# Two buffers for the forward decays of a state-space mixer, one in PSUM and one in SBUF, and a shared place for the turned gated output

## The reference, cut to what matters

```python
dt = softplus(einsum('blr,dr->bld', dt, dt_w) + dt_b)   # 256 channels
A = -exp(A_log)                                          # 256 channels x 16 states
dA = exp(dt[..., None] * A)                              # the decays
dBx = dt[..., None] * Bm[:, :, None, :] * xc[..., None]
# for each token: h = dA_t * h + dBx_t ; y = sum over the 16 states of h * C_t
y = (ys + xc * D) * silu(z)                              # the gated output
out = einsum('ble,ed->ble', y, out_w)
```

## Time and profile before

| | |
|---|---|
| median of 3 runs | 3504.08 us (3494.14 to 3508.31) |
| profiled execution | 3522.14 us, its span 3520.3 us |
| mean granted TensorE clock | 0.891 |
| busy over the span | PE 77%, DVE 73%, ACT 63%, POOL 60% |
| mixer's scans | about 1500 to 3122 us of the span |
| busy in the mixer | about 9 tenths for DVE, ACT and POOL in the page's slices, 8 for PE |

### The profile page before, as it was taken

The page is one execution under the profiler, slowest core; times in us unless marked ns, Lnnn a source line. Parts: engine busy times, 40 slices in busy tenths (PEclk is TensorE's granted clock), DMA queues, the critical chain, the costliest instruction groups (busy, mean ns, idle before and its releaser), DMA issues. The chain is left out here.

```text
span 3520.3 us, 56028 instructions
## 1 busy us (share of the span) xinstructions
PE 2719.5 (77%) x18635; PEld 2086.9 (59%) x18635; DVE 2575.9 (73%) x3474; ACT 2232.3 (63%) x3991; POOL 2114.0 (60%) x1427
## 2 busy tenths in 40 slices
PE   3999999322999920688888888888888887749994
PEld 2555555221999920256666666666666665639993
DVE  3788887443333357089999999999989999967893
ACT  1577776320222200498899898889989989746652
POOL 1233332464333312389998899898989989832565
PEclk6799999555999965799999999999999999879995
DMA  4455554212666654012222222222222222212222
GB/s 105 91 102 100 106 100 79 73 55 85 192 191 192 193 151 102 31 62 73 82 76 79 75 76 72 79 80 75 78 74 77 73 77 82 84 54 76 67 61 75
DMA packets 221906, 321.69 MB, mean 91 GB/s; under 512 B 37706, under 2 KB 133478, under 8 KB 216874
## 3 DMA queue, kind: packets, MB, share of 16 engines
q1 hardware_dynamic: 200322, 298.46, 30.6%
q0 software_dynamic: 12224, 18.29, 1.5%
q10 hardware_dynamic: 9072, 1.27, 0.3%
HBM read 269.84 MB, written 55.68 MB: 92 GB/s over the span
## 5 line engine op out<-in xcount | busy, mean ns | idle before, releaser
L1720 POOL TENSOR_TENSOR resid_x<-s_ux,s_B_rows 128x1024 f32<-128x1024 f32 x256 | 605.4, 2365 | 141.9 <-PE s_y L2080 141.3
L2000 DVE TENSOR_TENSOR_SCAN resid_x<-s_dA,resid_x 128x1024 f32<-128x1024 f32 x256 | 581.1, 2270 | 126.7 <-ACT s_dA L1811 123.4
L2008 DVE TENSOR_TENSOR_SCAN resid_x<-s_back_decay,s_back_in 128x1024 f32<-128x1024 f32 x256 | 583.4, 2279 | 55.5 <-ACT s_back_decay L1821 55.5
L2080 PE MATMUL s_y<-identity,resid_x 128*128 128x128 f32 x4096 | 553.9, 280 | 7.2 <-issue 6.4
L2080 PEld LDWEIGHTS s_y<-identity,resid_x 128*128 128x128 f32 x4096 | 493.8, 145 | 58.4 <-issue 36.0
L1728 POOL TENSOR_TENSOR resid_x<-resid_x,s_C_rows 128x1024 f32<-128x1024 f32 x192 | 454.5, 2367 | 4.0 <-DVE resid_x L2000 4.0
L2067 PE MATMUL s_back_in<-identity,resid_x 128*128 128x128 f32 x2048 | 293.1, 290 | 141.5 <-ACT resid_x L1832 74.1
L491 DVE TENSOR_REDUCE a_row_max<-a_maxscores 128x2 f32<-128x512 f32 x512 | 335.9, 684 | 87.9 <-PE a_maxscores L566 87.3
L2015 DVE TENSOR_TENSOR resid_x<-resid_x,s_C 128x1024 f32<-128x1024 f32 x320 | 382.3, 1195 | 14.0 <-PE s_C L2057 10.6
L1811 ACT ACTIVATE s_dA<-s_dt,s_A 128x510 f32<-128x510 f32 x512 | 330.0, 676 | 87.7 <-DVE resid_x L2000 87.5
L1832 ACT ACTIVATE resid_x<-s_uT,s_bT 128x256 f32<-128x256 f32 x864 | 368.8, 498 | 1.3
(11 more groups left out here) (391 smaller groups left out, 5349.2 us busy)
## 6 DMA issues: line engine op xcount, KB each, us to landing
s_B_rows<-forward_rows SPq DMA_DIRECT2D x256, 256.0 KB, 3.1
e_w<-L_ffn_w_by_expert SPq DMA_DIRECT2D x71, 768.0 KB, 4.8
s_C_rows<-forward_rows SPq DMA_DIRECT2D x192, 256.0 KB
a_Q<-split_qk SPq DMA_DIRECT2D x96, 192.0 KB
split_qk<-a_parts SPq DMA_DIRECT2D x32, 384.0 KB, 2.7
e_x<-slot_inputs SPq DMA_DIRECT2D x71, 130.0 KB
a_K<-split_qk SPq DMA_DIRECT2D x64, 128.0 KB
c_y<-choice_outputs SPq DMA_DIRECT2D x16, 512.0 KB, 6.7
```

What stands on the lines that cost most here:

```text
L1720: tt(R[s, 0], ux[par][:], brow[s % BRING][:].unsqueeze(1).broadcast_to([P, C2, W]), ALU.mult).then_inc(S["in_ready"], 1)
L2000: nc.vector.tensor_tensor_scan(r, a, r, 0.0, ALU.mult, ALU.add).then_inc(S["scanned"], 1)
L2008: nc.vector.tensor_tensor_scan(r[:, ::-1], a[:, ::-1], b[:, ::-1], 0.0, ALU.mult, ALU.add).then_inc(S["scanned"], 1)
L2080: last = mm(YP[:, t, c2 * P:(c2 + 1) * P], R[s, d][:, c2, t * P:(t + 1) * P], core.ident[:], is_transpose=True, start=((s, d) == (0, 1) an ...
```

## The change

The forward decays get two buffers, used in turn by even and odd states: the PSUM tile as before for even states and a new SBUF tile for odd states. ACT may now write the decays of a state once the forward scan of two states before has read that buffer. The first column of both buffers is set to zero at the start. The place for the new SBUF tile (4 KB in each partition) comes from `ygT`, which now lies in `ex`; so ACT's copies into `ygT` get one more wait, on the last read of that half of `ex` by POOL in the current pair (`off_corr`). The order of the instructions on each engine is the same as before, but for one more memset on DVE before the loop.

```diff
--- before.py
+++ after.py
@@ -1633,9 +1633,9 @@
         R = {(s, d): lots[:, 4 + s % 2 if d else s % 4] for s in range(DS) for d in range(DIRS)}
         bt = [core.X[:, k * C2 * W:(k + 1) * C2 * W].rearrange("p (n e) -> p n e", e=DI) for k in (6, 7)]
         yg = sb("y_gated", [P, G * TC, DI])
-        ygT = sb("y_gated_T", [P, C2, W])
+        ygT = ex
         o = sb("out", [P, G * TC, D])
-        dA = core.psum("s_dA", [P, C2, G, T], on=on)
+        dA = [core.psum("s_dA0", [P, C2, G, T], on=on), sb("dA1", [P, C2, G, T])]
         bP = core.psum("s_back_in", [P, C2, G, T], on=on)
         YP = core.psum("s_y", [P, G * TC, DI], on=on)
         CP = core.psum("s_C", [P, W], on=on)
@@ -1658,7 +1658,8 @@
             @block.vector
             def _(dve):
                 nc.vector.memset(xT[:], 0.0)
-                nc.vector.memset(dA[:, :, :, 0:1], 0.0)
+                for n in range(2):
+                    nc.vector.memset(dA[n][:, :, :, 0:1], 0.0)
                 nc.vector.memset(dec[0][:, :, :, T - 1:T], 0.0)
                 nc.vector.memset(dec[1][:, :, :, T - 1:T], 0.0).then_inc(S["pads"], 1)
                 dve.wait_ge(S["pads"], 1)
@@ -1806,9 +1807,9 @@
 
                     if s == 0:
                         act.wait_ge(S["dt_ready"], DIRS * C2 * j + C2)
-                    at(act, S["scanned"], CHUNKS * j + (2 * s - 1))
+                    at(act, S["scanned"], CHUNKS * j + (2 * s - 3))
                     for c2 in range(C2):
-                        last = func(dA[:, c2, :, 1:T], dt[par][:, 0, c2, :].rearrange("p (g t) -> p g t", t=T)[:, :, 1:T],
+                        last = func(dA[s % 2][:, c2, :, 1:T], dt[par][:, 0, c2, :].rearrange("p (g t) -> p g t", t=T)[:, :, 1:T],
                                     ACT.Exp, scale=Wt["A"][:, 0, c2, s:s + 1])
                     last.then_inc(S["dA_ready"], 1)
 
@@ -1886,8 +1887,10 @@
                     at(act, S["y_read"], i - 1)
                     func(z[u][:, 2 * h:2 * h + 2, :].rearrange("p n e -> p (n e)"), PR[:], ACT.Identity).then_inc(S["z_read"], 1)
 
-                def turned_back(j, c):
+                def turned_back(i, j, c):
                     act.wait_ge(S["yT_ps"], C2 * j + (c + 1))
+                    if live(i, 0):
+                        act.wait_ge(S["off_corr"], DIRS * C2 * i + (C2 + c + 1))
                     at(act, S["out_ps"], j)
                     func(ygT[:, c, :], PR[:], ACT.Copy).then_inc(S["yT_read"], 1)
 
@@ -1967,7 +1970,7 @@
                             for what in ACT_AT.get(c, ()):
                                 prep(i, u, what)
                         if c in (24, 26) and live(i, 2):
-                            turned_back(i - 2, (c - 24) // 2)
+                            turned_back(i, i - 2, (c - 24) // 2)
                         if c == 30 and live(i, 2):
                             j = i - 2
                             act.wait_ge(S["out_ps"], j + 1)
@@ -1996,7 +1999,7 @@
 
                     dve.wait_ge(S["dA_ready"], DS * j + (s + 1))
                     dve.wait_ge(S["in_ready"], DS * j + (s + 1))
-                    r, a = flat(R[s, 0]), dA[:].rearrange("p c g t -> p (c g t)")
+                    r, a = flat(R[s, 0]), dA[s % 2][:].rearrange("p c g t -> p (c g t)")
                     nc.vector.tensor_tensor_scan(r, a, r, 0.0, ALU.mult, ALU.add).then_inc(S["scanned"], 1)
 
                 def scan_back(j, s):
```

## The result

The changed kernel takes 3733.55 us (3725.65 to 3740.87), and before, on the same chip, 3499.11: a ratio of 1.0677, interval 1.065 to 1.0705. That is 234 us slower; 173 were predicted. The profiled execution has a span of 3739.0 us.

What follows compares the result with a forecast made beforehand. DVE was taken as nearest to full, 94.6 of 101.75 us a pair. POOL's 92.0, odd scans' 17.6 and 3 idle make 112.6, +10.9 in fifteen pairs, +9 in the last: +173, 3676 us; own range 3622 to 3737, widened to 3600 to 3760.

Steps and rivals of the forecast that it cites:

- The price of a second SBUF operand: Mixer, eight odd forward scans a pair: they and POOL exclude each other, adding 8 x 2.2 = 17.6 us to POOL's 92.0.
- Interleaving: Rival, odd scans: POOL uses the turns between a scan's elements, paying about 1.1 us a scan; 3490 us, chance 0.06.
- no contention: Rival, odd scans: no contention with POOL, so the second buffer pays about 55 us; 3449 us, chance 0.09.
- One that has waited is let in at POOL's next boundary: Odd scans on DVE: each waits only for POOL's current instruction, 0 to 2.3 us, about 1.1 in the mean.
- 3 us of idle time left on POOL: Each mixer pair: POOL, coming behind DVE, waits less for slots; idle time chosen as 3 us, between 0 and 9.7.
- exclusion without relief: Third rival: POOL's idle time stays whole as DVE's later scans delay slots; 17.6 us a pair, 3786 us, chance 0.09.
- DVE is no longer the fuller one; POOL is: Mixer pair: DVE rises to 103.4 us with its waits, POOL and odd scans together need 109.6.
- The floor of 109.6 us: Mixer pair: POOL's 92.0 us and the odd scans' 17.6 lie one after the other, +7.9 us against 101.75.
- The last pair: Last mixer pair, without preparation beside it: DVE sets the pace, 8 x 1.1 = 9 us added.
- Relief counted as nothing: Mixer: the second buffer's gain, at most 82.4 us of DVE waits, counts for nothing, as ACT's lateness hides behind POOL.
- What was taken at no cost: One memset, ACT's odd decays written to SBUF (0.5 us a pair, covered), and ACT's wait on off_corr: nothing added.
- signs named for the profile: Odd scans 2.27 to 4.6 us, forward mean 2.8, POOL products lengthened, POOL above 95%, ACT's wait gone, pair 112 to 113.

Runs made afterwards that it cites:

- e1: The changed kernel with ACT's old wait, odd decays written to SBUF only after the forward scan of the state before: 1.0659 of before, 3773 us.
- e3: Against the kernel before, the single forward-decay buffer lies in SBUF, so all 16 forward scans of a pair read two SBUF tensors: 1.1152, 3928 us.
- e5: The changed kernel with POOL waiting once a pair, before its products at c=24, for the forward scan of state 13: 1.0518 of before, 3717 us.
- e4: The changed kernel with each POOL instruction in the mixer first waiting on POOL's own instruction before it: 1.0636 of before, 3761 us.
- e8: Against the kernel before, only state 12 uses the SBUF buffer, and ACT writes state 13's decays one state earlier: 1.0000, 3492 us.
- e2: The kernel before with only ygT laid over ex and its new wait on off_corr, one PSUM buffer for the decays: 1.0003 of before.
- e6: The changed kernel with the SBUF buffer used for states 1, 3 and 5 alone, all others in PSUM: 1.0071 of before.
- The repeated run: The changed kernel run again without alteration, beside other experiments on the same chip: 1.0666 of before, a pair 116.96 us.

## Why the prediction was right, and where its size was off

- **The price of a second SBUF operand** was the right step. The scan, which no row before had shown in that position, is kept out whole and keeps POOL out whole; e1, e3 and e5 tie the loss to it. It is what the Trainium skill says on "SBUF — State Buffer", section "Who interferes with whom", of any DVE instruction with two SBUF inputs, and the trace agrees: POOL's product of 1.04 us takes 3.05. That section also lets the order of issue decide which one waits, and the prediction took this over; in the trace it is not always so, since five POOL products issued after a scan went ahead of it. Interleaving would have left POOL 1.1 us longer and DVE as it was; no contention would have left both as they were. Both fall.
- **"One that has waited is let in at POOL's next boundary"** is the step that failed. It held in 69 of 99 cases at the first boundary with POOL back to back, and in 1 of 51 at a later one. This made DVE's wait 2.17 us in the mean, not 1.1, and DVE's busy time 112.6 us in a pair, not 103.4. e4 shows the step apart: with no scan passed over the wait is 0.95 us and DVE's busy time 102.7.
- **"3 us of idle time left on POOL"** is the term of the sum that was too small: 116.96 - 109.6 leaves 7.4 us, and 15 x 4.4 = 66 us is the whole of the miss of 61. The reason for 3, that POOL comes behind DVE and waits less for slots, did not hold: it waited 9.3 us a pair, as before. With state 13 let in (e5) it waited 4.5 us a pair (60.5 in 1500) and 3.0 are left of the pair, so a part of this idle time hangs on the scans that are passed over. With 9.3 us a pair the sign came that the prediction named for a miss in size, a wait for L2080 (now L2083) that stays near 136 us, and with it most of the third rival, exclusion without relief. That rival gave 282 us more, the forecast 173, and the measured 234 lies between, a little nearer to the rival. The range held because its upper end, 3737 before it was widened, allowed for 7 us of idle time on POOL, not because the waits were foreseen.
- **"DVE is no longer the fuller one; POOL is"** was wrong for the same reason: DVE 96% busy, POOL 90%. With no scan passed over (e4) it is true, 88% and 94%.
- **The floor of 109.6 us** held: no version with eight such scans was below it in the mean of its pairs, and the one with sixteen lies at its own.
- **The last pair**: +9 predicted, +8.0 measured; its eight odd scans wait 7.7 us in all.
- **Relief counted as nothing**: right in the changed kernel (e1). Whether it would pay without exclusion stays open: no run has two buffers in PSUM; e8, with one exclusion a pair, got nothing from it.
- **What was taken at no cost**: right. e2 shows it for the wait on `off_corr`. The added memset takes 62 ns in the trace, and ACT's decays into SBUF 709 ns where those into PSUM take 671.
- Of the signs named for the profile, the even and odd lengths, POOL's second length and ACT's vanished wait came as told. The mean of L2003 was 3.35, not 2.8; the longest scan 13.2, not 4.6; POOL not above 95%; a pair took 117, not 112 to 113.

## What to carry to other kernels

Before giving a tile on DVE's input side a place in SBUF, look whether that instruction's other input lies in PSUM and how busy POOL is; with both inputs in SBUF its time and POOL's add up, and the sum per period is a floor to reckon with first. Such an instruction can wait for many of POOL's, not for one, so look at its longest and not only at its mean, and at the state in which it falls. And see what an earlier wait hides before counting its removal: here the single buffer cost DVE 82 us of waiting, but in both attempts to free them with few scans in SBUF (e6, e8) DVE waited about as long before other instructions.

## What the runs showed of the hardware that I had not expected

A DVE instruction that waits for POOL can be passed over again and again. Over the changed kernel's 128 odd scans: when POOL's next instruction began 0.14 us or more after its last one ended (a wait of its own, as between L1744 and L1750), the scan was let in, 37 times of 37. In e4_pool_gaps 0.08 us was enough, 41 times of 41. When POOL ran back to back, the scan was let in 69 times of 99 at the first boundary, and once passed over there, 1 time of 51 at any later one. The repeated run gives 39 of 39, 67 of 97 and 1 of 51, e3_all_in_sbuf 90 of 90, 95 of 125 and 1 of 79.

What decides the first boundary stays open. The time between the scan's issue and POOL's end doesn't separate the two (both outcomes at 0.67 to 0.83 us), and scan 12 of e8_sbuf_state_12 was let in each time. It hangs on the place in the pair: in the changed kernel every scan that was passed over is of state 11, 13 or 15. Where L1721 ends and L1744 follows back to back, the scan of state 5 was let in 15 times of 15 and that of state 11 passed over 14 times of 14, at the same 0.7 us after its issue among others.
